# A decoder layer on one core: query rows by DMA, maxima turned in 128 columns, probabilities as the stationary operand

## The reference

```python
scores = einsum('bhqd,bhkd->bhqk', Q, K) / sqrt(8)
# first attention: scores * tau[..., None] + delta[:, :, None, :]
# second attention: where(mask, -1e15, scores)
attn = softmax(scores, axis=-1)
out = einsum('bhqk,bhkd->bhqd', attn, V)       # then transposed, reshaped, and linear(out)
x = x + out
```

## Time and profile before

| | |
|---|---|
| median of 3 runs | 303.44 us (303.01 to 304.27) |
| the profiled execution | 304.08 us, its span 302.3 us |
| TensorE busy | 284.5 us, 94% of the span, 1675 products |
| weight loads | 203.1 us, 67% |
| VectorE, ScalarE, GpSimd busy | 76%, 64%, 61% |
| TensorE's granted clock, mean | 0.993 of full speed |

### The profile page before, as it was taken

One profiled execution on the slowest core, in us unless ns is written; L12 is line 12 of the kernel. 1 busy time (PEld: TensorE's weight loads), 2 busy tenths in 40 slices (PEclk: granted clock), 3 DMA queues, 4 the chain that ended last, 5 costly groups with the idle time before them and its releaser, 6 DMA issues.

```text
span 302.3 us, 5347 instructions
## 1 busy us (share of the span) xinstructions
PE 284.5 (94%) x1675; PEld 203.1 (67%) x1675; DVE 228.2 (76%) x512; ACT 192.6 (64%) x352; POOL 184.0 (61%) x262
## 2 busy tenths in 40 slices
PE   1999999999999999899889999999999999999994
PEld 1734576666655565456665788888888888888883
DVE  3896798799859886987896559789956676676664
ACT  2797747796884566456742797766655555555552
POOL 8240062097708870985177799999975665665661
PEclk9999989999999999999999999999999999999999
DMA  7920535457577243350000637666333353344321
GB/s 260 266 44 1 192 71 150 105 125 254 102 187 136 64 104 98 87 132 10 2 1 25 203 107 223 198 200 188 129 102 137 105 173 128 124 133 134 119 62 37
DMA packets 30636, 37.18 MB, mean 123 GB/s; under 512 B 5136, under 2 KB 19856, under 8 KB 30608
## 3 DMA queue, kind: packets, MB, share of 16 engines
q1 hardware_dynamic: 30608, 36.84, 42.2%
HBM read 28.43 MB, written 3.93 MB: 107 GB/s over the span
## 4 chain that ended last, share of the span: by engine, by line
PE 83%; DVE 9%; ACT 4%; DMA 2%; issue 2%; SPq 0%; ACTq 0%; DVEq 0%
PE bank L474 57%; PE bank L813 5%; PE bank L815 5%; PE bank L814 5%; PE bank L619 2%; PE bank L594 2%; PE bank L637 2%; DMA pa<-pack_a 2%; DVE rawmax L1214 2%; PE bank L606 1%; PE bank L480 1%; ACT conv L891 1%; PE bank L642 1%; PE bank L603 1%; ACT conv L922 1%
## 5 line engine op out<-in xcount | busy, mean ns | idle before, releaser
L1779 POOL TENSOR_TENSOR qbd<-vs,qbd 128x512 fp32r<-128x512 f32 x65 | 83.7, 1291 | 33.3 <-ACT qbd L1093 33.3
L474 PE MATMUL bank<-khl,stacks 128*128 128x512 f32 x396 | 101.4, 392 | 1.9 <-DVE vs L1575 1.9
L474 PEld LDWEIGHTS bank<-khl,stacks 128*128 128x128 f32 x396 | 73.6, 188 | 18.6 <-issue 3.7
L1606 DVE TENSOR_TENSOR conv<-bank,conv 128x512 f32<-128x512 f32 x60 | 41.5, 691 | 31.4 <-ACT bank L1057 28.3
L1057 ACT ACTIVATE bank<-bank 128x512 f32<-128x512 f32 x61 | 35.5, 582 | 43.9 <-PE bank L474 43.9
L1214 DVE TENSOR_REDUCE rawmax<-bank 128x4 f32<-128x512 f32 x64 | 43.3, 684 | 9.4 <-PE bank L474 8.4
L1093 ACT ACTIVATE qbd<-vs 128x512 fp32r<-128x512 f32 x65 | 40.6, 625 | 7.1 <-DVE vs L1583 4.6
L1614 DVE TENSOR_TENSOR vs<-conv,bank 128x512 f32<-128x512 f32 x61 | 41.9, 687 | 2.1
L474 PE MATMUL bank<-stacks 128*128 128x512 f32 x96 | 41.5, 482 | 1.1 <-DVE stacks L1524 0.6
L981 ACT ACTIVATE conv<-bank 128x512 f32<-128x512 f32 x64 | 35.1, 597 | 6.4 <-PE bank L474 5.6
L1743 POOL TENSOR_TENSOR stacks<-ring,stacks 128x384 fp32r<-128x384 f32 x33 | 33.7, 1021 | 1.4
(11 more groups left out here) (227 smaller groups left out, 431.6 us busy)
## 6 DMA issues: line engine op xcount, KB each, us to landing
conv<-coefficient_rows SPq DMA_DIRECT2D x122, 128.0 KB, 2.9
ring<-w SPq DMA_DIRECT2D x33, 192.0 KB, 3.6
stacks<-stacks SPq DMA_DIRECT2D x68, 64.0 KB, 2.1
split_rows<-stacks SPq DMA_DIRECT2D x6, 256.0 KB, 2.6
stacks<-split_rows SPq DMA_DIRECT2D x16, 96.0 KB
split_rows<-khl SPq DMA_DIRECT2D x3, 512.0 KB, 4.3
stacks<-split_rows SPq DMA_DIRECT2D x8, 192.0 KB
pa<-pack_a SPq DMA_DIRECT2D x1, 706.0 KB, 5.3
```

The lines of the kernel that those rows point to most:

```text
L474: return pe.matmul(out, lhsT, rhs, start=start, stop=stop)
L1606: dve.tensor_tensor(out, gate, spread[:, n % ROWS, :, :], ALU.mult).then_inc(gate_scaled, 1)
L1779: pool.tensor_tensor(hlo[:, n % 4, :].rearrange("p (b t) -> p b t", b=4), hx[n % 4], hhi[:, n % 4, :].bitcast(F32).rearrange("p (b t) -> p ...
```

## The change

The query rows of `qbd` no longer come through the array: SP's DMAs copy them from `qst` for every step but the first, a pass behind the key blocks. `turn_max` then turns the maxima alone, once, in 128 columns; `queries_with_max` copies 8 rows of each quarter, repeated over the four groups. In the value products the operands change places: the probabilities (128 columns) are the stationary operand and a head's values and one (9 columns) are moved, so that the output has queries on partitions and 9 columns for each head, in bank 4 (bank 7 for the last step). `copy_o`, `turn_out` and `oT` go; `norm` reads the output where it is. `pv(s-1, 3)` stands behind `scoresT(s, 0)`.

```diff
+        def attended(s):
+            return bank[4 if s < STEPS - 1 else 7][:, 0:H * (DK + 1)].rearrange("p (h c) -> p h c", h=H)
+        def turned(s, r):
+            if s == 0:
+                return bank[5][r, :].rearrange("p (g t) -> p g t", g=G)
+            return bank[5][r, 0:P].unsqueeze(1).broadcast_to([S_MAX, G, P])
...
+            def query_rows(s):
+                b = s % B
+                if s < 4:
+                    sp.wait_ge(qst_ready, G)
+                elif s < B:
+                    sp.wait_ge(rows_got[1][2 if s < 6 else 3], 64)
+                else:
+                    sp.wait_ge(qst_ready, G + 2 * (b // 4) + 2)
+                    sp.wait_ge(qst_odd, 2 * (b // 4) + 2)
+                wait(sp, scoredT, G * (s - 1))
+                for j in range(J):
+                    sp.dma_start(qbd[32 * j + S_MAX:32 * j + 32, s % 2, :, j, :].bitcast(F32),
+                                 qst[32 * j + S_MAX:32 * j + 32, :, b, :].bitcast(F32)).then_inc(qbd_rows[s % 2], 16)
...
+                if s > 1:
+                    query_rows(s - 1)
                 move_rows(s)
...
             # turn_max
+                if s > 0:
+                    pe.wait_ge(max_split, s + 1)
+                    mm(bank[5][:, 0:P], negmax[:, :], identr[:, :]).then_inc(max_turned, 1)
+                    return
...
             # scoresT
                     pe.wait_ge(qbd_ready, s + 1)
+                    if s > 0:
+                        pe.wait_ge(qbd_rows[s % 2], 16 * J * ((s + 1) // 2))
...
             def pv(s, g):
                 i = G * s + g
                 pe.wait_ge(exped, i + 1)
-                if g == 0:
-                    wait(pe, o_copied, s)
+                if g == 0 and s < STEPS - 1:
+                    wait(pe, normed, s)
+                elif g == 0:
+                    pe.wait_ge(scores_ready, 1)
                 for j in range(J):
-                    last = mm(bank[4][32 * j:32 * j + DK + 1, P * g:P * g + P], vs[s // B][:, s % B, J * g + j, :],
-                              probs[:, i % 8, j, :])
+                    h = J * g + j
+                    last = mm(attended(s)[:, h, :], probs[:, i % 8, j, :], vs[s // B][:, s % B, h, :])
                 last.then_inc(pv_done, 1)
-
-            def turn_out(s):
-                pe.wait_ge(o_copied, s + 1)
-                wait(pe, residual, s)
-                for g in range(G):
-                    last = pe.transpose(bank[6][:, P * g:P * g + P], oT[:, g, :], ident)
-                last.then_inc(o_turned, 1)
...
                     pv(s - 1, 2)
-                    pv(s - 1, 3)
+                    if not early:
+                        pv(s - 1, 3)
...
                     scoresT(s, 0)
+                if s >= 1 and early:
+                    pv(s - 1, 3)
...
-                if s >= 1 and making is None:
-                    turn_out(s - 1)
...
-            def copy_o(s):
-                act.wait_ge(pv_done, G * s + G)
-                wait(act, o_turned, s)
-                act.activation(oT[:, :, :].rearrange("p g t -> p (g t)"), bank[4][:, :], ACT.Copy)\
-                    .then_inc(o_copied, 1)
...
             # queries_with_max, on ScalarE and VectorE
+                rows = 32 if s == 0 else S_MAX
-                    r = slice(32 * j, 32 * j + 32)
+                    r = slice(32 * j, 32 * j + rows)
...
             def norm(s):
-                dve.wait_ge(o_turned, s + 1)
-                o = bank[6][:, :].rearrange("p (h c) -> p h c", h=H)
+                dve.wait_ge(pv_done, G * s + G)
+                o = attended(s)
```

More of the change, by code:

```diff
@@ L97, in decoder_layer @@
         nwt = sb("nwt", [P, 4, B])
-        oT = sb("oT", [P, G, P])
-        foldq = oT[:, 0:3, :]
+        foldq = sb("foldq", [P, 3, P])
         foldb = sb("foldb", [P, 2])
@@ L223, in decoder_layer @@
         kbd_ready = [sem(f"kbd_ready{i}") for i in range(2)]
+        qbd_rows = [sem(f"qbd_rows{i}") for i in range(2)]
         picks_ready = sem("picks_ready")
@@ L228, in decoder_layer @@
         const_ready = sem("const_ready")
-        (scored, maxed, max_split, max_turned, qbd_high, qbd_ready, scoredT, exped, pv_done, o_copied, o_turned, normed,
+        (scored, maxed, max_split, max_turned, qbd_high, qbd_ready, scoredT, exped, pv_done, normed,
          on_turned, on_copied, projected, residual) = (sem(n) for n in (
-             "scored", "maxed", "max_split", "max_turned", "qbd_high", "qbd_ready", "scoredT", "exped", "pv_done", "o_copied",
-             "o_turned", "normed", "on_turned", "on_copied", "projected", "residual"))
+             "scored", "maxed", "max_split", "max_turned", "qbd_high", "qbd_ready", "scoredT", "exped", "pv_done",
+             "normed", "on_turned", "on_copied", "projected", "residual"))
         logits_done = sem("logits_done")
@@ L431, in _ @@
                     load(pair)
+            query_rows(STEPS - 1)
             def coefficient_rows(n):
@@ L625, in pv @@
                 pe.wait_ge(exped, i + 1)
-                if g == 0:
-                    wait(pe, o_copied, s)
+                if g == 0 and s < STEPS - 1:
+                    wait(pe, normed, s)
+                elif g == 0:
+                    pe.wait_ge(scores_ready, 1)
                 for j in range(J):
-                    last = mm(bank[4][32 * j:32 * j + DK + 1, P * g:P * g + P], vs[s // B][:, s % B, J * g + j, :],
-                              probs[:, i % 8, j, :])
+                    h = J * g + j
+                    last = mm(attended(s)[:, h, :], probs[:, i % 8, j, :], vs[s // B][:, s % B, h, :])
                 last.then_inc(pv_done, 1)
-            def turn_out(s):
-                pe.wait_ge(o_copied, s + 1)
-                wait(pe, residual, s)
-                for g in range(G):
-                    last = pe.transpose(bank[6][:, P * g:P * g + P], oT[:, g, :], ident)
-                last.then_inc(o_turned, 1)
             def turn_on(s):
                 pe.wait_ge(normed, s + 1)
+                wait(pe, residual, s)
                 pe.transpose(bank[6][:, 0:P], on[:, :, :].rearrange("p h d -> p (h d)"), ident)\
@@ L757, in _ @@
                     scoresT(s, 3)
-                if making is not None:
-                    turn_out(s - 1)
                 if making is not None:
@@ L799, in _ @@
             pe.wait_ge(exped, G * STEPS)
-            pe.wait_ge(o_copied, STEPS)
+            pe.wait_ge(normed, STEPS - 1)
             products(0)
@@ L988, in queries_with_max @@
                 for j in range(J - 1 if s < B else 2):
-                    r = slice(32 * j, 32 * j + 32)
-                    last = act.activation(qbd[r, s % 2, :, j, :], bank[5][r, :].rearrange("p (g t) -> p g t", g=G),
-                                          ACT.Copy)
+                    r = slice(32 * j, 32 * j + rows)
+                    last = act.activation(qbd[r, s % 2, :, j, :], turned(s, r), ACT.Copy)
                 last.then_inc(qbd_high, 1)
@@ L1025, in _ @@
                                    scale=-1.0).then_inc(scores_ready, 1)
-                if s >= 1:
-                    copy_o(s - 1)
                 if s in (0, 2):
@@ L1228, in queries_with_max @@
                 for j in range(J - 1 if s < B else 2, J):
-                    r = slice(32 * j, 32 * j + 32)
-                    last = dve.tensor_copy(qbd[r, s % 2, :, j, :], bank[5][r, :].rearrange("p (g t) -> p g t", g=G))
+                    r = slice(32 * j, 32 * j + rows)
+                    last = dve.tensor_copy(qbd[r, s % 2, :, j, :], turned(s, r))
                 last.then_inc(qbd_ready, 1)
             def norm(s):
-                dve.wait_ge(o_turned, s + 1)
-                o = bank[6][:, :].rearrange("p (h c) -> p h c", h=H)
+                dve.wait_ge(pv_done, G * s + G)
+                o = attended(s)
                 link(dve.reciprocal(rec[:, :].unsqueeze(2), o[:, :, DK:DK + 1]))
```

## The result

The changed kernel takes 372.8 us in the median (364.9 to 380.7, 4 runs) against 303.75 (303.0 to 304.3); the ratio is 1.2017, 95% interval 1.1982 to 1.2052. It is slower by a fifth. Its executions fall in two groups: at a mean granted clock of 0.867 they took 365 us, at 0.833 they took 381; the ratio is that of the first group, the profiled execution (380.65 us, span 378.9) is of the second, and what parts them isn't settled.

A forecast was written before the change was run, and what follows sets the result against it. TensorE was taken to bound the kernel, VectorE the tail of rounds. With the clock falling, 38 + 32 + 10 + 2 = +82 us on 304.1, less 0.6, gave 385 us; 328 to 405 held all but about 0.15.

The forecast's parts named there:

- The value products' price: 32 value-product pairs a round, paced by 128-column loads: 0.111 us each at 2.4 GHz, +2.45 us a round; about 0.22 at 1.2 GHz.
- The delta row: Profile row of delta products, 128x128 loaded and 16 columns moved, 0.111 us each, taken as nearest to the new value products.
- Rival 4: Value products' 128-column loads hide behind one another, below 0.045 us a pair: 294 to 299 us, not slower; chance 0.03.
- The sum at 2.4 GHz, +32: Attention rounds at full clock: +1.8 x 6, +2.1 x 9 and 2 for round 16, +32 us in all.
- `turn_out`, put at nothing: Four transposes a round, 0.48 us, inside the tail VectorE sets: no gain in plain rounds, bounds 0 and 0.3 us.
- `turn_max`, -0.35 us x 15: From round 1 the query product goes and the maxima's product shrinks: together 0.35 us a round, counted fully.
- The clock: TensorE's clock falls in the attention stage under many loaded and few moved columns: +82 us in all, 385 us likeliest.
- rival 2: The clock falls in the first attention only: +59 us, 362 us; chance 0.14 including seldom falls in the second.
- Rival 1: The clock stays high through attention, since falls come from waits between matmul bursts: 335.5 us, bounds 328 and 342; chance 0.32.
- The SP step: Four query-row DMAs a round on SP's queue: 2.5 us more, 8.4 in the worst round, covered in rounds of 7 us and more.

The follow-up runs named there:

- Values only ten times over: Kernel before with only the value products' operands swapped and their 9 columns moved 10 times over, no query-row DMAs: 335.4 us, ratio 1.1041.
- the kernel without DMAs: Kernel before with maxima turned in 128 columns and 8-row casts, value products as before, query-row DMAs and their waits left out: 302.9 us, ratio 0.9974.
- Rows only: Kernel before with query rows by SP's DMAs, maxima turned in 128 columns and 8-row casts; value products, `copy_o` and `turn_out` as before: 338.3 us, ratio 1.112.

## Why the prediction was right, step by step

The side, the mechanism and the shape of the clock's row came as predicted; the sum was +82 and the measured cost is +61 to +77 us, so the likeliest time, 385 us, is over every execution, and the range held. The terms:

- **The value products' price.** Predicted 0.111 us a pair at 2.4 GHz and 0.22 at 1.2; measured 0.106 and 0.205. The delta row was the right one to go by. The Trainium skill's rule that a load costs by its columns ("TensorE: Matmul & The Clock Gate", "LDWEIGHTS (loading the stationary operand)"), 0.107 us by the estimate, agrees with the trace at 2.4 GHz; at 1.2 GHz a pair takes twice that, 0.205 us. Rival 4 (pairs that hide behind one another, under 0.045) is out.
- **The sum at 2.4 GHz, +32.** Values only ten times over gives +31.8 without the thin turning. The swap, with `turn_out` and `copy_o` gone, was put at about 2.15 x 6 + 2.45 x 8 + 4.4 = 37 us by the prediction's terms. Measured are 12.3 in rounds 1 to 6 (12.9 put down), 15.1 in rounds 7 to 14 (19.6) and 4.5 behind them (334.1 - 170.53 against 302.3 - 143.19). In the masked round the swap costs 8.47 - 6.35 = 2.12 us, 0.33 less than 2.45; what gives that back wasn't told apart (`turn_out`, put at nothing, is the candidate at 0.48). Rounds 7 and 11 got only 1.4 and 1.5 us. In the first attention the plain round shown got 7.74 - 5.29 = 2.45, the most of the six; their mean is 2.05, near the 2.15 put down.
- **`turn_max`, -0.35 us x 15.** Mis-sized: 0.8 us in place of 5.3. "Together 0.35 us a round, in the dense part, so they count fully" was the wrong sentence, and not in the plain rounds, which in the kernel without DMAs gained 0.26 and 0.33 us each in the mean: what they gained was lost again in rounds 7 and 11 (0.7 us each) and behind the last turning (1.3), places that the sum didn't look at. This error and the one before are of opposite sign; that the +32 is as near as it is is luck.
- **The clock.** "The clock falls in the attention stage" held, in both attentions, and rival 2 (first attention only) is out. The ground for it was thin, one fall at 42 us: in the changed kernel the same delta products, from 37.54 to 40 us, left the clock at 1.00 until 50, and in 9 of the 35 executions of the kernel before that ran beside the experiments the mean clock is 0.999 or 1.000, which leaves hardly any room for that fall. The forecast was right, but its row doesn't carry it; the experiments do. The plain first-attention round at 1.2 GHz was put at 11.6 us and took 11.78, with two small errors against each other (the value products 6.4 us and not 7.0, the rest 5.4 and not 4.6). But the clock came back for stretches there, at 85 us and at 95, so rounds 1 to 6 cost +31.4 and not +38. Rounds 7 to 14 were put at 6 x 4.5 + 10 = 37 and cost 33.4; what lies behind them was put at 6.5 and cost 12.5, since the clock stayed under full for most of 207 to 235 us (0.62). (The 7.9 us of a masked round double to 15.8 and not to 15.5, which changes nothing.)
- **Why it falls.** Rival 1 went by waits between bursts. With the same instructions, loads and queues, moving 90 columns in place of 9 takes 31.2 us away and holds 1.00 through both attention windows, and in the changed kernel 9, 36 and 90 columns give mean clocks of 0.83 to 0.87, 0.87 to 0.91 and 0.965 to 0.985. TensorE had no pause from 130.5 to 172 us, and the clock fell in it. So here many loaded and few moved columns are enough. The Trainium skill's section "HAM oscillation" of the same page, which puts falls down to waits, fits other falls of these runs, such as the one at 104 us with 90 columns, behind 4.67 us of waiting; it doesn't fit the one at 146 us of the changed kernel, and for the one at 50 us, behind a stretch with idle time, either would do.
- **The SP step.** "2.5 us more a round", "late, by some 1 to 3 us in a few early rounds": wrong in size. It is 3.35 us more, and the 8.1 in all, near the 8.4 put down for the worst round, is that of a usual one; in rounds as short as before it costs 35 us. I took the price of a key block's issue for that of a query block's, and I didn't lay out SP's order at step 7, which alone is 6 us. "In rounds of 7 us and more [...] that is covered" held only under the low clock: without the DMAs the changed kernel is no faster within its spread. With 90 columns moved and rounds of 7 to 8.5 us, the thin turning and the DMAs cost 347.1 - 335.4 = 11.7 us (8 by the ratios), and there it didn't hold.

So the change's 61 to 77 us are 32 for loads of 128 columns in place of 9, and the rest, 29 to 45, for what the clock does under them. Rows and maxima (35 us alone) are hidden behind both, but for some 5 us that the spread leaves open. None of the versions that ran with the swap or the DMAs comes near the kernel before; the only one not behind it is the shorter turning with its DMAs left out, 302.9 us, and that one doesn't move the query rows at all.

## What to carry to other kernels

The price of an operand as the stationary one went here by its column count times the number of products, with 9 columns moved as with 90. Read it from any row that loads as many columns, and then look in a trace for what the clock does where few columns are moved for each load, because that cost as much again here. When work goes from an engine to DMAs, multiply the issues by the time of one and hold the queue's sum against the round, in its order, at every point where another transfer is ahead. And test each part alone: here a part that costs 35 us by itself costs nothing that can be seen in the whole, and 8 to 12 us of it came back when 90 moved columns kept the clock nearer to full.

## What was unexpected of the hardware

- Moving ten times the columns made the kernel faster by 31.2 us (366.6 to 335.4), and the clock was the higher one where TensorE was the less busy: 44.85 of 48.17 us in rounds 1 to 6, against 66.41 of 67.52.
- The kernels that move 9 columns for each load of 128 spread from one execution to the next: 364.9 to 380.7 us, 363.5 to 373.6, 360.0 to 381.0. Those at a mean clock of 0.987 and more spread by 0.7% at most (302.4 to 304.4 and 335.1 to 335.9). Rows only, at 0.94 to 0.96, spreads no more (336.8 to 338.7), so a low clock alone doesn't make the spread.
- A DMA issue from ScalarE's queue holds ScalarE's own work for 0.8 us, as long as one from SP's holds SP. The price of an issue isn't one number: 0.84 us for a query block's, 0.63 to 0.75 for the key blocks shown, 0.45 for the moved rows shown (and up to 0.85 in the earlier trace rows).
